# A two-layer decoder on one NeuronCore: folding two weight matrices during the mixture-of-experts steps instead of during the linear attention, and other moves around that seam

## What is computed

```
x = x + self_attention(ln(x))         # 16 heads, q and k normalised per head
x = x + cross_attention(ln(x), ctx)   # 16 heads
x = x + experts(ln(x))                # 8 experts, the best 2 of each row, softmax weights
x = x + linear_attention(ln(x))       # see below
x = x + cross_one_head(ln(x), ctx)    # one head of width 256, with biases
x = x + quantised_ffn(ln(x))          # fp8 rounding of x and of the weight
```

```
# linear attention (16 heads of 16)
q = norm(relu(q)+1e-6); q = norm(q**3); k likewise
kv = einsum('bhnd,bhne->bhde', k, v)
z = 1 / (einsum('bhnd,bhd->bhn', q, k.sum(axis=2)) + 1e-6)
out = einsum('bhnd,bhde,bhn->bhne', q, kv, z)
out = out + depthwise_conv3(out)      # along the rows: left, middle and right tap, bias
return out @ w_proj.T + b_proj
# one-head cross attention
query = x @ Wq + bq; key = ctx @ Wk + bk; value = ctx @ Wv + bv
return softmax(query @ key.T / 16) @ value
```

## Time and profile before

| | us |
|---|---|
| median of 3 runs | 1662.14 (1662.04 to 1662.39) |
| the profiled execution | 1662.17 |
| its span, first to last instruction | 1660.3 |

### The profile page before, as it was taken

One profiled execution on the slowest core, in us unless ns is written; L12 is line 12 of the kernel. 1 busy time (PEld: TensorE's weight loads), 2 busy tenths in 40 slices (PEclk: granted clock), 3 DMA queues, 4 the chain that ended last, 5 costly groups with the idle time before them and its releaser, 6 DMA issues. The chain is left out here.

```text
span 1660.3 us, 36679 instructions
## 1 busy us (share of the span) xinstructions
PE 1585.8 (96%) x14540; PEld 641.6 (39%) x14540; DVE 1481.6 (89%) x2152; ACT 1313.1 (79%) x2558; POOL 417.4 (25%) x671
## 2 busy tenths in 40 slices
PE   6999999999999999999999999999998999889997
PEld 3542222322233222323322222222224576757773
DVE  6899999999999999998999999999975887688876
ACT  4618999879988989898899999999995565635644
POOL 5801110111321412310311111111003455533302
PEclk9999999999999999999999999999999999999999
DMA  4001001001100210110221100101002000024551
GB/s 149 14 7 20 14 15 14 14 14 20 34 14 14 38 29 14 20 27 14 64 79 14 27 14 19 23 14 27 8 8 90 1 2 1 1 42 93 95 104 51
DMA packets 148026, 52.33 MB, mean 32 GB/s; under 512 B 137424, under 2 KB 146128, under 8 KB 147600
## 3 DMA queue, kind: packets, MB, share of 16 engines
q1 hardware_dynamic: 147152, 48.62, 14.3%
q10 hardware_dynamic: 704, 1.38, 0.2%
HBM read 14.07 MB, written 2.10 MB: 10 GB/s over the span
## 5 line engine op out<-in xcount | busy, mean ns | idle before, releaser
L968 DVE TENSOR_REDUCE mxp<-ps_m 128x2 f32<-128x1024 f32 (+2 forms) x928 | 1049.0, 1195 | 41.4 <-PE ps_m L747 40.0
L897 ACT ACTIVATE work<-ps_s 128x512 f32<-128x512 f32 x1856 | 1001.7, 598 | 76.6 <-PE ps_s L771 48.9
L797 PE MATMUL ps_av<-work,vst 128*32 128x256 f32 x7424 | 592.8, 391 | 14.7 <-ACT avs L904 12.3
L771 PE MATMUL ps_s<-qb,k_stack 50*128 50x512 f16 x1856 | 565.6, 382 | 0.5 <-ACT v_rows L915 0.3
L747 PE MATMUL ps_m<-k_stack,qa 48*128 48x512 f16 (+1 forms) x2048 | 534.3, 358 | 2.3 <-PEq L1123 0.5
L797 PEld LDWEIGHTS ps_av<-work,vst 128*32 128x32 f32 x7424 | 147.0, 108 | 383.2 <-ACT work L897 321.6
L771 PEld LDWEIGHTS ps_s<-qb,k_stack 50*128 50x128 f16 x1856 | 119.6, 94 | 378.6 <-ACT work L897 321.3
L747 PEld LDWEIGHTS ps_m<-k_stack,qa 48*128 48x128 f16 x2048 | 108.2, 93 | 21.5 <-DVE mxp L968 14.8
L616 POOL TENSOR_SCALAR mtmp<-negm 128x16 f32<-128x16 f32 x32 | 8.2, 255 | 390.4 <-DVE negm L973 390.3
L602 POOL COPY vst<-v_rows 128x1024 f32<-128x1024 f32 (+1 forms) x32 | 30.6, 956 | 144.4 <-PE ps_av L797 144.3
L682 POOL TENSOR_TENSOR q_rows<-avs,rc 128x256 f32<-128x256 f32 x31 | 19.2, 620 | 173.2 <-DVE rc L979 173.2
(11 more groups left out here) (441 smaller groups left out, 1985.5 us busy)
## 6 DMA issues: line engine op xcount, KB each, us to landing
x_res<-in_x SPq DMA_DIRECT2D x4, 512.0 KB, 8.1
w_experts<-in_w_experts SPq DMA_DIRECT2D x1, 2048.0 KB, 8.1
out<-x_res SPq DMA_DIRECT2D x8, 256.0 KB, 2.1
v_rows<-in_ctx_c SPq DMA_DIRECT2D x1, 1664.0 KB, 7.2
work<-in_ctx_t SPq DMA_DIRECT2D x1, 1456.0 KB, 15.6
ctx_n<-in_ctx_n SPq DMA_DIRECT2D x1, 1248.0 KB, 7.8
w_qkv<-in_w_qkv ACTq DMA_DIRECT2D x1, 768.0 KB, 8.5
w_qkv<-in_w_qkv SPq DMA_DIRECT2D x1, 768.0 KB, 4.2
```

The lines of the kernel that those rows point to most:

```text
L771: pe.matmul(ps_s[:, bank, :], STACKS[part(n)][rows, group(n) * PAIRS + j, t * P:t * P + P], qb[n % 2][rows, :, j, :], start=True, stop=Tru ...
L797: m = pe.matmul(ps_av[32 * h:32 * h + 32, cols], vst[n % 2][:, t, h, :], pbuf[(tau[n] + t) % 2][:, h, cols], start=(t == 0 and half == 0), ...
L897: a.activation(pbuf[g % 2][:, h, :], ps_s[:, b, :], ACT.Exp, scale=factor).then_inc(s["exp"], 1)
L968: v.tensor_reduce(dst, src, AX.X, ALU.max).then_inc(s["mred"], 1)
```

## The change

It moves the making of the fold into the experts' steps. TensorE makes the keys' product in steps 2 and 3, the bias in step 4, the side in step 4; the turned maxima in step 16 and their spread in step 17. ScalarE copies the unscaled products out of PSUM in step 5 (`hold_fold`) and scales the fold at the end (`scale_fold`). VectorE takes the three maxima in steps 9 to 11, those over rows in step 17, and `scales` in step 18. GpSimd makes `wide` in step 2, where it now waits for the loads, as TensorE does. The products stand in `ps_kv`, which `outer(0)` overwrites, so it waits for the copies.

Other moves: ScalarE has a dummy square root in step 15 (`warm`); the roots of the last two norms stand behind other work in steps 16 and 17. The bias b_proj of tiles 13 to 15 is added in the linear attention instead of in the experts' steps. `outer(13)` stands behind the keys of tile 15. In the linear attention windows 3 and 4 take their left taps as ScalarE product and GpSimd sum, as the others do; `project(0)` and `project(1)` stand one transpose earlier, `query_first` stands behind `project(5)`, `first_low` behind `add(6)`, and three idle products stand at the end of TensorE's list.

```diff
@@ projection_experts_queries
+    HELD = 13
+    SCALED, FOLDED = 14, 17
+        ps_f, ps_side, ps_b = ps_kv[:, 0, :].rearrange("p (k n) -> p k n", k=2), ps_kv[:, 1, 0:D + 1], ps_kv[:, 1, 260:262]
+        ps_t, ps_w = logit[0:3, 264:264 + P], logit[:, 400:403]
@@ gpsimd
-                if f == 0:
+                if n == 2:
                     g.wait_ge(loads[0], 16 * len(loads[1]))
+                    g.tensor_tensor(wide[:, :, :], ones[:, :].unsqueeze(1).to_broadcast([P, 2, P]),
+                                    bk[:, :].unsqueeze(2).to_broadcast([P, 2, P]), ALU.mult).then_inc(s["rep"], 1)
                 if f == T - 1:
-                    plus(f)
                     key_shares(f)
                     query_cubes(f)
...
-                if f is not None and f < T - 1:
+                if f is not None and f < HELD:
                     plus(f)
@@ tensor
+            def folded_keys(n):
+                if n == 0:
+                    pe.wait_ge(loads[0], 16 * len(loads[1]))
+                for j in range(2):
+                    m = pe.matmul(ps_f[:, n, :], wq_t[:, j, n * P:n * P + P], wk_t[:, j, :], start=(j == 0), stop=(j == 1))
+                m.then_inc(s["made"], 1)
...
+            def turned_peaks():
+                pe.wait_ge(s["gused"], T)
+                pe.wait_ge(s["fold"], 3)
+                pe.transpose(ps_t, peak[:, :], ident[:, :]).then_inc(s["made"], 1)
+
+            def spread_peaks():
+                pe.wait_ge(s["fold"], 5)
+                pe.matmul(ps_w, ones[0:3, :], diag[:, :], start=True, stop=True).then_inc(s["made"], 1)
+
             def outer(f):
+                if f == 0:
+                    pe.wait_ge(s["held"], 3)
...
+                if n == 4:
+                    folded_bias()
                 if n < T:
                     experts(n, 2)
...
                 if n + 1 < T:
                     logits(n + 1)
+                if n in (2, 3):
+                    folded_keys(n - 2)
+                if n == 4:
+                    folded_side()
                 if n < T:
                     experts(n, 3)
+                if f == T - 1:
+                    outer(f - 2)
                 if f is not None:
                     values(f, c)
                 if f == T - 1:
                     last_queries(f, c)
-                if n - LAG - 1 >= 0:
+                if n == T:
+                    turned_peaks()
+                if n == T + 1:
+                    spread_peaks()
+                if n - LAG - 1 >= 0 and f != T - 2:
                     outer(n - LAG - 1)
@@ scalar
+            def hold_fold():
+                e.wait_ge(s["made"], 4)
+                e.copy(fold[:, :, :], ps_f).then_inc(s["held"], 1)
+                e.activation(side[:, 0:D + 1], ps_side, ACT.Copy, scale=1.0 / 16.0).then_inc(s["held"], 1)
+                e.copy(raw[:, :], ps_b).then_inc(s["held"], 1)
+
+            def scale_fold():
+                e.wait_ge(s["fold"], SCALED)
+                e.activation(fold[:, :, :], fold[:, :, :], ACT.Copy, scale=part[:, 0:1]).then_inc(s["scaled"], 1)
...
                 if n < T:
                     weigh(n, 1)
+                if n == T - 1:
+                    e.activation(warm[:, :], gain[:, :], ACT.Sqrt)
...
                     focused_rows(f + 1)
+                if n == T:
+                    root(FOCUSED_NORMS, 3, s["fvar"], s["froot"])
                 if n + 1 >= T and focused(n + 1) is not None:
                     copy_pair(c + 1, 2, 4)
                 if f is not None:
                     squared(f)
+                if n == T + 1:
+                    root(FOCUSED_NORMS, 4, s["fvar"], s["froot"])
...
-                if n >= T - 1 and norm_at(FOCUSED_NORMS, n) is not None:
-                    root(FOCUSED_NORMS, norm_at(FOCUSED_NORMS, n), s["fvar"], s["froot"])
+                if n == 5:
+                    hold_fold()
...
+            scale_fold()
             squared_last()
@@ vector
+                    if 9 <= n <= 11:
+                        peak_of(n - 9)
...
                     if n == T + 1:
                         focused_norm_back(len(FOCUSED_NORMS) - 1)
+                        peaks_over_rows()
+                    if n == T + 2:
+                        scales()
@@ linear_attention, tensor
-            folded_keys()
             pe.wait_ge(s["set"], 5)
             numerators(0)
             numerators(1)
-            folded_bias()
...
+            for p in range(6):
+                turn(p)
+                numerators(p + 2)
+            project(0)
             turn(6)
-            project(0)
+            project(1)
             turn(7)
-            project(1)
             project(2)
             project(3)
             turn_first()
             project(4)
+            project(5)
             query_first()
-            project(5)
             project(6)
             project(7)
+            idle_products(pe, ps_n[:, 1, 0, 0:D], ident[:, :], w[:, 0, :], 3)
@@ linear_attention, scalar
-            middle(3, 0)
-            middle(3, 1)
+            window_taps(3)
             out(7)
-            middle(4, 0)
-            middle(4, 1)
+            window_taps(4)
             a.wait_ge(s["var"], 1)
@@ linear_attention, gpsimd
+            for n in range(HELD, T):
+                g.tensor_tensor(x[:, n, :], x[:, n, :], bias[:, :], ALU.add).then_inc(s["bias"], 1)
-            for i in range(LATE):
+            for i in range(len(WINDOWS)):
                 left(i, 0)
                 left(i, 1)
-                right(i)
+                if i < SPLIT:
+                    right(i)
@@ linear_attention, vector
             norm_back()
-            left(3, 0)
-            left(3, 1)
             v.wait_ge(s["pad"], 1)
             right(3, 0)
             right(3, 1)
             add(3)
-            left(4, 0)
-            left(4, 1)
             right(4, 0)
             right(4, 1)
             add(4)
             add(5)
+            add(6)
             first_low()
-            add(6)
             add(7)
```

More of the change, by code:

```diff
@@ L1451, in projection_experts_queries @@
 def projection_experts_queries(prog, x, st, tmp, qf, wo, bo, gate, weh, wel, gain, iota, w, ps_kv, ident, loads,
-                               ctx_gain, ctx_n, vh, after):
+                               ctx_gain, ctx_n, vh, after, ones, wq_t, wk_t, bq, bk, fold, side, near, undo, wf, wf_peak):
     nc = prog["nc"]
@@ L1465, in projection_experts_queries @@
         "fsum", "fvar", "froot", "frows", "xf", "qk", "vv", "vout", "relu", "sq", "cube", "sums", "rs", "k", "q", "kv", "ones", "vh",
-        "last_q", "last_relu", "last_sq", "plus")}
+        "last_q", "last_relu", "last_sq", "plus", "rep", "made", "held", "fold", "scaled")}
     s_made, s_free = ([fresh(prog, f"p{k}{i}") for i in range(4)] for k in ("made", "free"))
@@ L1483, in projection_experts_queries @@
         v_ring, k_ring = [sb(f"pv{r}", [P, 2, P + 1]) for r in range(RING)], [sb(f"pk{r}", [P, D]) for r in range(RING)]
+        warm = sb("pwarm", [P, 1])
+        wide, raw, peak, top, diag = sb("pwide", [P, 2, P]), sb("praw", [P, 2]), sb("ppeak", [P, 3]), sb("ptop", [3, 1]), sb("pdiag", [3, 3])
+        bound, floor, scale, back, part = (sb(f"p{k}", [P, 1]) for k in ("bound", "floor", "scale", "back", "part"))
         turn_wf = cx.enter_context(nc.psum_tensor("pturn_wf", [P, 4, P], F32))
@@ L2053, in norm_variance, with linear_attention @@
     return v.scalar_tensor_tensor(tmp[:, 1, cols], tmp[:, 0, cols], 0.25, tmp[:, 1, cols], ALU.mult, ALU.add)
-def linear_attention(prog, x, st, qt, ps_kv, tap, tap_bias, w, mask, ident, ones, wq_t, wk_t, bq, bk, fold, side, near, undo,
-                     ctx_gain, wf, wf_peak, mean, rstd, tmp, first):
+def linear_attention(prog, x, st, qt, ps_kv, tap, tap_bias, w, bias, mask, ident, fold, near, mean, rstd, tmp, first):
     nc = prog["nc"]
-    s = {k: fresh(prog, "la_" + k) for k in ("set", "pad", "tap1", "num", "rz", "o", "to", "ot", "mid", "lt", "left", "late", "rt", "conv",
-                                             "convg", "prod", "x", "st", "rep", "made", "fold", "side", "scaled", "norm", "var", "root",
+    s = {k: fresh(prog, "la_" + k) for k in ("set", "pad", "tap1", "num", "rz", "o", "to", "ot", "lt", "left", "rt", "conv",
+                                             "convg", "prod", "bias", "x", "st", "norm", "var", "root",
                                              "rs", "xn", "xtr", "xcp", "qm", "qh", "ql")}
@@ L2077, in linear_attention @@
         ot, yt, lt, rt = sb("lot", [P, 2, S + 2]), sb("lyt", [P, 2, S]), sb("llt", [P, 2, 512]), sb("lrt", [P, 512])
-        wide, peak, top, diag = sb("lwide", [P, 2, P]), sb("lpeak", [P, 3]), sb("ltop", [3, 1]), sb("ldiag", [3, 3])
-        bound, floor, scale, back, part = (sb(f"l{k}", [P, 1]) for k in ("bound", "floor", "scale", "back", "part"))
         ps_n = cx.enter_context(nc.psum_tensor("lpsn", [P, 2, 2, 512], F32))
@@ L2102, in _ @@
         def _(pe):
-            def folded_keys():
```

(30 more changed lines are left out.)

136 lines of the change are left out of this document (57 added, 79 removed).

## The result

The changed kernel takes **1670.07 us**, the median of 6 runs (1667.44 to 1671.66), beside 1662.09 (1660.54 to 1663.98, also 6) for the kernel before on the same chip: a ratio of 1.0045 with a 95% interval of 1.0032 to 1.0058, which is 5.3 to 9.6 us. The forecast was 1666.0, with a range up to 1668.8. The sign is right; the loss is 7.5 us (by the ratio) instead of 3.9.

A forecast was written before the change was run, and what follows sets the result against it. TensorE was taken to bound the experts' steps from the seventh on, ScalarE then VectorE most of the linear attention. +2.8 + 4.5 - 3.1 - 0.35 = +3.85 on the median 1662.14 gave 1666.0 us, range 1661.0 to 1668.8.

The forecast's parts named there:

- Step 1: Experts' steps: the fold adds 4.0 us on TensorE, partly filling waits, plus ScalarE copies: +2.8 (bounds +0.8 and +4.7).
- Step 2: Tail, steps 15 to 17: table load +1.4, a 3.2 us wait for the spread maxima; step 18 starts 3.1 later.
- rival (d): Tail: the warm root loads no table, the load stays where it was, 1.8 of waits stay: 1666.4; chance 0.03.
- Step 3: Clock: TensorE falls to 1.2 GHz behind the tail's 3.2 us wait: +1.4 (bounds 0 and 1.7).
- Step 4: Tail, steps 18 to 22: `scales` delays and the moved last keys give +0.4, a faster cube gives -0.4.
- Step 6: After the linear attention: idle products fill 0.65 of a 2.23 wait, first scores run at full clock: -0.35.
- Step 5: Linear attention: ScalarE takes VectorE's place as the bound; the end comes at 1465.5 instead of 1468.7: -3.1.
- Rival (b): Early waits absorb nearly all the fold (+0.8), ScalarE's root in the linear attention not late: 1662.0 or 1659.3; chance 0.12.
- Rival (c): Tail worse: `scales` meets GpSimd and takes 2.74, relus late, early waits fill nothing: 1668.7; chance 0.15.
- rival (a): Clock holds at 2.4 GHz behind both new waits, -1.4 in the tail, -1.3 in the linear attention: 1663.3; chance 0.25.

The follow-up runs named there:

- e4_filled: The changed kernel with nine idle products in front of the next stage's first transposes, where TensorE waits 4.17 us: 1666.49 us, ratio 1.0030 to the kernel before.
- e3_pool_cut: The changed kernel with GpSimd's three additions of the third tap window cut to 8 columns each (output not the reference's): 1668.85 us, ratio 1.0045.
- e9_bias_later: The changed kernel with GpSimd's bias rows starting only when VectorE has written the block-diagonal operands: 1669.18 us, ratio 1.0049.
- e10_no_idle: The changed kernel with all costs named by the runs taken out, but without the seven idle products added in the combined run: 1659.61 us, ratio 0.9989.
- e6_left_back: The changed kernel with the late windows' left taps back on VectorE and the norm's front after the third sum, as before: 1666.67 us, ratio 1.0034.
- e8_all: The changed kernel with later maxima spread, table load, fold copy and bias rows, left taps and norm as before, seven idle products: 1659.69 us, ratio 0.9991.
- e1_spread_later: The changed kernel with the spread of the maxima at the end of step 18 instead of 17 and the scales in step 19: 1665.36 us, ratio 1.0021.
- e2_warm_later: The changed kernel with step 15's dummy square root, and so the table load, placed later, just ahead of the waiting weighing: 1668.96 us, ratio 1.0043.
- e5_rest_alone: The kernel before with every edit of the change except the move of the fold, which stays in the linear attention: 1664.72 us, ratio 1.0017.

## Why the prediction was right in sign and short by half

**Step 1** (fold in the experts' steps): right, 2.66 for 2.8: the waits of the early steps took up the rest of the 4.0. **Step 2**: the wait of step 15 is 1.26, with its hidden 0.16 the 1.4 of the rows; the table is loaded there, which rules out rival (d). The Trainium skill, "ScalarE: Activation LUTs", section What ACT_TABLE_LOAD costs, adds a drain to the load, by which this would have been 2.8 (estimate of the page). The trace doesn't agree: the square root follows 0.01 after the load. The wait for the maxima is 3.42 for 3.2, the product behind it 0.31 for 0.15. Together +3.61 for +3.1. **Step 3**: four groups of matmuls behind it take 1.77 longer than their like before, for 1.4, over 3.3 us at 0.52. **Step 4**: nothing, as summed: `scales` (twelve operations, not the seventeen of the prediction) took 1.60 without the stretched `undo` (0.15), TensorE waited 0.29 at the transposes of step 18 to 20 instead of 0.8, and 0.62 for GpSimd's key shares at 1435.30 instead of 1.16. **Step 6**: -0.50 for -0.35, the first scores at granted 1.00.

**Step 5** is the one that failed, by 2.9 of the 3.45 us. Its mechanism was right, ScalarE in VectorE's place: the root is at 24.85 after the attention's start, forecast 24.45. The stage's end was mis-sized in three terms:

- *The clock, 1.7.* The step let four couples be projected at 1.73 each "from there", which is full clock, behind a wait that its own terms make 3.6 us long. In the kernel before, TensorE was through the projections ahead of the transposes at 1457.04 (1458.18 less the wait of 1.14, below); the step moved VectorE's sums 4.9 earlier (1450.38 to 1445.5), so 1452.2, and the transposes came to 1455.8. Step 3 had found half clock behind waits of 2.2 to 2.4 and applied it to two places; the longest wait of all, at this third place, was not held against it. `e4_filled` prices it: 1.67. The two rows of the kernel before:

```profile
1450.38 0.69 DVE L2327 TENSOR_TENSOR x_res<-lprod,x_res 128x512 f32<-128x512 f32 x1 [1.49 <-PE lprod L2160]
```

```profile
1458.18 0.44 PE L2167 MATMUL lpsn<-ident,oxn 128*128 128x128 f32 x2 [1.14 <-DVE oxn L2343]
```

- *VectorE held up, 0.7 of the 1.48 between root and transposes.* The prediction took 0.8. When the root came, VectorE was still in the third sum, because the norm's front had taken 3.8 us instead of 0.8. `e3_pool_cut` shows the cause and a price of 0.55.
- *The root, 0.4.* The bias rows on GpSimd were given "0, at most +0.7". They cost 0.62 at once (`e9_bias_later`), on the operation that the numerators wait for. The half clock behind that wait cost 0.25 less than forecast, so the first output copy was at 5.56 instead of 5.15.

The last two are one oversight. The Trainium skill, "SBUF — State Buffer", section Who interferes with whom, states that VectorE and GpSimd share a pair of ports as an exclusive lock, and that a VectorE instruction with two SBUF inputs, or a `tensor_scalar` in its two-port mode, can be shut out by GpSimd for a whole instruction. The traces agree: 0.98 against 0.36 and 1.23 against 0.17, with and without GpSimd's additions beside them. (0.83 for a cube of 0.42) and the earlier trace rows (1.25) showed such operations before; the prediction used these rows to say where a slow operation would go away. Which quick ones the moved GpSimd work would now meet it asked only for the bias rows, as a bound, and not for the sums of the taps beside the norm's front.

Rival (b), ahead of the kernel before, needed ScalarE's root not to be late; it was. Rival (c), 1668.7, is nearest to the measured 1670.07, for the wrong reason: its `scales` never met GpSimd.

**What stays open.** The terms above explain one execution of 1668.19. The median is 1.9 higher: four of the six executions took 1669.9 to 1671.7, with a mean granted clock of 0.994 where the other two have 0.995. That points to more time at half clock in them, but no trace shows where. By the chip's ratios the rest of the change without the fold costs 2.8 us; its trace shows 1.9, counted from the stage's start. Which part of a stretch behind a wait runs at half clock changes from kernel to kernel (5.09 behind 4.17, 6.31 behind 4.16, 5.31 behind 3.61, for the same sixteen products; more in the last section), so a single trace sizes such a term to about 1 us only.

## What to carry to other kernels

Work that is moved onto the engine that hardly waits costs all that its remaining waits don't take up (here 2.66 of 4.0 us), and gains elsewhere only as far as the next bound of that stage: list, for the stage that is to gain, every engine's time at the point where they meet, and hold each wait that results against the waits behind which this trace shows the lower clock. Small VectorE operations on the way to a matmul want GpSimd quiet: one wait of GpSimd took 0.6 us off them here, though the kernel got no faster by it alone (`e9_bias_later`). And where the engine that hardly waits must consume a small reduction that nothing needs soon, let it do so a step after the reduction is made: 4 us hung on that one step.

## What the runs showed of the hardware

A long wait on TensorE didn't decide the clock behind it by its length alone. In `e10_no_idle` two waits are 2.39 us; the sixteen numerators behind the first ran at 0.50, the sixteen projections behind the second at 1.00:

```profile
1432.91 4.00 PE L2210 MATMUL lpsn<-lbd,q_rows 128*128 128x136 f32 x16 [2.39 <-DVE lbd L2416]
...
1456.74 0.44 PE L2239 MATMUL lpsn<-ident,oxn 128*128 128x128 f32 x2 [2.39 <-DVE oxn L2401]
1457.01 3.96 PE L2232 MATMUL lprod<-w_proj,lyt 128*128 128x256 f32 x16
```

```profile
1432.90:1436.70 3.80, 3.79 (x16) 3.79 (x17) 1.08 (x3) 0.00 (x0) 2.09 (x3) 0.50 0.00 0
1457.00:1460.60 3.60, 3.49 (x18) 2.79 (x16) 3.57 (x10) 0.37 (x1) 0.00 (x0) 1.00 0.00 0
```

The same pair shows in two other runs: numerators of 4.00 behind 2.38 in `e9_bias_later`, projections of 3.96 behind 2.40 in `e6_left_back`. What differs ahead of them: before the first, TensorE had waited 1.17 us shortly earlier (0.75 in `e9_bias_later`); before the second it had been busy for 10 us. No run here separates that from other differences. Half clock was also seen without a long wait: in the last stage of the kernel before, TensorE waited 1.39, 1.05 and 0.73 ahead of its transposes at 1640.84, 1643.06 and 1645.29, and from 1644 to 1648 its granted clock is 0.50.

Nor does the code decide it. Up to the wait for the maxima the changed kernel and `e3_pool_cut` have the same instructions, and the wait is the same within 0.01 us. The two groups of matmuls behind it, of the changed kernel and then of `e3_pool_cut`:

```profile
1419.41 1.82 PE L1661 MATMUL pbank<-pxo,w_qkv 128*128 128x128 f32 x8
1421.02 1.91 PE L1655 MATMUL pbank<-w_qkv,pxo 128*128 128x256 f32 x4
```

```profile
1419.60 0.38 PE L1707 MATMUL plogit<-pdiag,ones 3*128 3x3 f32 x2 [3.43 <-DVE pdiag L2053]
1419.91 0.71 PE L1715 MATMUL ps_kv<-pv,pk 128*128 128x129 f32 x4
1420.46 1.06 PE L1661 MATMUL pbank<-pxo,w_qkv 128*128 128x128 f32 x8
1421.35 1.03 PE L1655 MATMUL pbank<-w_qkv,pxo 128*128 128x256 f32 x4
```

Half clock in one execution, full in the other. That alone puts the attention of `e3_pool_cut` 1.6 us earlier (180.91) in its trace. Three more runs have the same instructions up to there:

| us | wait | from the product to the next step's outer product |
|---|---|---|
| the changed kernel | 3.42 | 5.36 |
| `e4_filled` | 3.42 | 5.35 |
| `e6_left_back` | 3.42 | 5.38 |
| `e9_bias_later` | 3.43 | 5.38 |
| `e3_pool_cut` | 3.43 | 3.70 |

So behind this wait half clock came in four executions of five and cost 1.7 us each time. A forecast has to carry it as a likely outcome and not as a certain one: of rival (a), the half for the tail was true in one of these executions. The rival's other half, full clock behind the wait for the numerators, was true in none: behind waits of 2.38 to 3.01 the numerators took 3.10 to 4.00 in all eight kernels that have such a wait, where full clock gives 2.02. The wait of 1.50 in `e8_all` was followed by full clock, as that of 1.48 in the earlier trace rows; all six waits of 3.6 us and more for the normed rows (the changed kernel, `e1_spread_later`, `e2_warm_later`, `e3_pool_cut`, `e5_rest_alone`, `e9_bias_later`) were followed by slower matmuls, of 4.83 to 6.31 us where 3.62 is the full pace.
